# Attention with all softmax row sums made on TensorE, and the next heads' loads issued by ScalarE

## The reference

```
xn = layernorm(x)
q, k, v = split(clip(xn @ Wqkv.T, -8, 8))           # 32 heads of 32
q, k = layer_norm(q)*w + b, layer_norm(k)*w + b
scores = q k^T / sqrt(32) + slope[h] * (key - query); causal mask
probs = softmax(scores);  attn = (probs @ v) @ Wout.T
out = x + attn + xn @ (mean|W| * sign(W)).T + bias
```

## Time and profile before

| what | value |
|---|---|
| three runs | 1596.76, 1600.59, 1603.05 us |
| median | 1600.59 us |
| profiled execution, its own time | 1595.62 us |
| its span, first to last instruction | 1593.8 us |
| mean granted TensorE clock | 0.957 of full |
| PE busy | 1420.4 us (89%) |
| DVE busy | 731.8 us (46%) |
| POOL busy | 615.8 us (39%) |
| ACT busy | 571.5 us (36%) |

### The profile page before, as it was taken

The page is one execution under the profiler, slowest core; times in us unless marked ns, Lnnn a source line. Parts: engine busy times, 40 slices in busy tenths (PEclk is TensorE's granted clock), DMA queues, the critical chain, the costliest instruction groups (busy, mean ns, idle before and its releaser), DMA issues.

```text
span 1593.8 us, 24481 instructions
## 1 busy us (share of the span) xinstructions
PE 1420.4 (89%) x9256; PEld 655.4 (41%) x9256; DVE 731.8 (46%) x1246; ACT 571.5 (36%) x1081; POOL 615.8 (39%) x380
## 2 busy tenths in 40 slices
PE   4899999999999979999988878888988888797998
PEld 2455445444545434444333333333433333233443
DVE  6665355545454311267655555555655555301111
ACT  4443133323333200005555545555555555530000
POOL 4221122222222100003555556666555555666443
PEclk9999999999999989999999999999999999899999
DMA  6453232322232372211222221122222221024543
GB/s 234 152 165 113 66 79 59 79 60 72 67 79 59 93 200 79 80 53 48 69 69 62 65 57 46 47 69 69 70 69 69 62 65 28 17 85 158 158 145 119
DMA packets 145396, 136.85 MB, mean 86 GB/s; under 512 B 83744, under 2 KB 112416, under 8 KB 145120
## 3 DMA queue, kind: packets, MB, share of 16 engines
q1 hardware_dynamic: 79264, 118.92, 25.4%
q10 hardware_dynamic: 66048, 16.78, 4.9%
HBM read 93.06 MB, written 42.47 MB: 85 GB/s over the span
## 4 chain that ended last, share of the span: by engine, by line
PE 56%; POOL 25%; issue 12%; ACT 3%; DMA 2%; DVE 1%; SPq 1%; POOLq 0%; ACTq 0%; DVEq 0%
PE ps L979 38%; POOL arena L588 21%; PE ps L1115 4%; PE ps L1054 4%; PE ps L1138 3%; PE ps L1143 2%; PE ps L1032 2%; ACT arena L721 2%; PE ps L1148 2%; POOL arena L567 1%; PE ps L1057 1%; POOL small L530 1%; DMA v_scr<-arena 1%; PE ps L1118 1%; ACT arena L729 1%
## 5 line engine op out<-in xcount | busy, mean ns | idle before, releaser
L979 PE MATMUL ps<-arena 128*128 128x512 f16 x3584 | 795.9, 382 | 28.7 <-DVE arena L857 9.8
L979 PEld LDWEIGHTS ps<-arena 128*128 128x128 f16 (+1 forms) x3584 | 349.8, 98 | 446.1 <-issue 13.5
L588 POOL TENSOR_TENSOR arena<-arena 128x2048 f32<-128x2048 f32 (+1 forms) x96 | 330.6, 3444 | 473.2 <-ACT arena L721 466.1
L886 DVE TENSOR_REDUCE arena<-ps 128x1 f16<-128x512 f32 (+3 forms) x768 | 380.1, 551 | 282.7 <-PE ps L1057 247.5
L721 ACT ACTIVATE arena<-ps 128x512 f32<-128x512 f32 (+3 forms) x768 | 332.4, 493 | 170.2 <-PE ps L1118 77.8
L1115 PE MATMUL ps<-arena 128*128 128x512 f16 (+3 forms) x768 | 252.2, 337 | 113.6 <-ACT arena L721 111.9
L1054 PE MATMUL ps<-arena 127*128 127x512 f16 (+3 forms) x768 | 240.3, 334 | 0.0
L1115 PEld LDWEIGHTS ps<-arena 128*128 128x128 f16 x768 | 75.4, 99 | 288.6 <-ACT arena L721 189.3
L857 DVE TENSOR_SCALAR arena<-ps 128x1024 f32<-128x1024 f32 x48 | 58.8, 1225 | 253.4 <-PE ps L979 226.1
L1138 PE MATMUL ps<-arena 128*32 128x512 f32 (+3 forms) x1536 | 163.9, 508 | 0.4 <-ACT arena L729 0.2
L555 POOL TENSOR_TENSOR arena<-arena 128x1024 f16<-128x1024 f32 x32 | 68.0, 2125 | 125.4 <-ACT arena L698 125.4
(11 more groups left out here) (51 smaller groups left out, 873.6 us busy)
## 6 DMA issues: line engine op xcount, KB each, us to landing
arena<-in_x SPq DMA_DIRECT2D x32, 512.0 KB, 4.5
arena<-in_wqkv_t SPq DMA_DIRECT2D x48, 256.0 KB, 4.0
base_scr<-arena SPq DMA_DIRECT2D x16, 512.0 KB, 2.8
q_scr<-arena ACTq DMA_DIRECT2D x16, 512.0 KB, 4.1
k_scr<-arena ACTq DMA_DIRECT2D x16, 512.0 KB, 4.4
arena<-k_scr SPq DMA_DIRECT2D x16, 512.0 KB
arena<-q_scr SPq DMA_DIRECT2D x32, 256.0 KB
v_scr<-arena SPq DMA_DIRECT2D x16, 512.0 KB, 2.9
```

The lines of the kernel that those rows point to most:

```text
L588: nc.gpsimd.tensor_tensor(acc[:, :, at:HALF], former, p32[k % PSLOTS][:, :, 0:w], ALU.add)\
L886: ins = nc.vector.tensor_reduce(negm[s % 2][:, at:at + 1], ps[:, NATB[use(s, pos) % RB], col:col + width], AX, ALU.max, negate=True)
L979: ins = nc.tensor.matmul(dst[c], lhs(k, a), wparts[:, k, b, c * HALF:(c + 1) * HALF], start=(k == 0 and (a, b) == order[0]), stop=(k == KT ...
```

## The change

- GpSimd's additions, `acc` and their semaphore are gone. `with_v` multiplies every chunk's exponentials with the ones; the product with `acc` is gone.
- The loads of V and of the stack leave SP. ACT issues them: V of group n+1 behind (2, 3), and the seven parts of the stack of group n+2 one per chunk, behind (3, 3) to (9, 3).
- ACT's `o_high` of the first half moves from (0, 3) to (2, 0), `os_copy` of the second half from (2, 0) to (2, 1), `o_high` of the second half from (8, 1) to (9, 0).
- The tables `NATS` and `PV_AFTER` are new.

```diff
-        acc = f32(at, PW).rearrange("p (j q) -> p j q", j=GH); at += PW
...
-        NATS = [4, 3, 3, 2, 5, 4, 4, 4, 5, 4, 2, 2]
+        NATS = [3, 4, 3, 2, 5, 5, 3, 4, 4, 4, 3, 2]
...
-        PV_AFTER = {(1, 0): [-2], (2, 0): [-1], (2, 3): [0], (4, 2): [1], (5, 2): [2], (6, 2): [3],
...
+        PV_AFTER = {(0, 3): [-2], (2, 1): [-1], (3, 0): [0], (4, 2): [1], (5, 2): [2], (6, 2): [3],
+                    (7, 1): [4], (7, 3): [5], (8, 3): [6], (9, 3): [7, 8], (11, 0): [9]}
...
-        def load_stack(eng, n):
+        LOADS = 7
+
+        def load_part(eng, n, part):
...
             for n in range(STACKS):
-                load_stack(sp, n)
+                for part in range(LOADS):
+                    load_part(sp, n, part)
...
-                    if n < GROUPS - 1:
-                        load_vg(sp, n + 1)
-                    if n + 2 < GROUPS:
-                        sp.wait_ge(st_done, NC * GH * n)
-                        load_stack(sp, n + 2)
...
-            def add_in(n, c):
...
-                nc.gpsimd.tensor_tensor(acc[:, :, at:HALF], former, p32[k % PSLOTS][:, :, 0:w], ALU.add)\
-                  .then_inc(add_done, 1)
-
             for n in range(GROUPS):
                 for c in range(NC):
-                    if not DIRECT[c] and CHUNKS[c][1] > 1:
-                        add_in(n, c)
...
                     need(act, pv_done, k - PSLOTS + 1)
-                    need(act, add_done, adds_for(k - PSLOTS))
...
+                            if (c, j) == (2, 3) and n < GROUPS - 1:
...
+                                load_vg(act, n + 1)
+                            if j == 3 and 3 <= c < 3 + LOADS and n + 2 < GROUPS:
+                                load_part(act, n + 2, c - 3)
...
-                if DIRECT[c]:
-                    for j in range(GH):
-                        ins = nc.tensor.matmul(dst(S_BANK, j, at), ones_w, p[:, j, 0:w],
-                                               start=first, stop=last and qb == 0)
-                if last and qb == 1:
-                    pe.wait_ge(add_done, ADDS * (n + 1))
-                    for j in range(GH):
-                        ins = nc.tensor.matmul(dst(S_BANK, j, 0), ones_w, acc[:, j, :], start=False, stop=True)
+                for j in range(GH):
+                    ins = nc.tensor.matmul(dst(S_BANK, j, at), ones_w, p[:, j, 0:w], start=first, stop=last)
```

More of the change, by code:

```diff
@@ L337, in load_stack @@
             hk = k_scr[h0:h0 + GH, :, toks].rearrange("j r t -> r j t")
[L338 to L342, removed]
-                cols = slice(a * HALF, (a + 1) * HALF)
-                eng.dma_start(qs[s][0:2 * DH, a], hq[:, :, cols]).then_inc(stack_ld[s], 16)
-                eng.dma_start(qs[s][2 * DH:3 * DH, a], hq[0:DH, :, cols]).then_inc(stack_ld[s], 16)
+            if part == 0:
+                dst, src = ks[s][0:DH], hk[0:DH]
+            elif part == 1:
+                dst, src = ks[s][DH:3 * DH], hk
+            elif part == 2:
+                dst, src = ks[s][3 * DH:3 * DH + 3], k_extra[h0:h0 + GH].rearrange("j r t -> r j t")
+            else:
+                a, again = (part - 3) // 2, (part - 3) % 2
+                cols = slice(a * HALF, (a + 1) * HALF)
+                if again:
+                    dst, src = qs[s][2 * DH:3 * DH, a], hq[0:DH, :, cols]
+                else:
+                    dst, src = qs[s][0:2 * DH, a], hq[:, :, cols]
+            eng.dma_start(dst, src).then_inc(stack_ld[s], 16)
         def stack_loaded(n):
-            return 16 * 7 * (n // STACKS + 1)
+            return 16 * LOADS * (n // STACKS + 1)
         def load_vg(eng, n):
@@ L477, in _ @@
                     sums_out(blk_no(n - 1, 1))
-                    if n == 1:
-                        for s in range(2):
-                            sp.wait_ge(v_st[s], stored(NT // 2))
-                    if n < GROUPS - 1:
-                        load_vg(sp, n + 1)
-                    if n + 2 < GROUPS:
-                        sp.wait_ge(st_done, NC * GH * n)
-                        load_stack(sp, n + 2)
                 if n < GROUPS - 1:
@@ L577, in o_low @@
                 nc.gpsimd.tensor_tensor(part[1], os_sb[m % 2][:, 0, :], part[0], ALU.subtract).then_inc(ol_done, 1)
-            def add_in(n, c):
-                qb, t, at, w = span(c)
-                k = n * NC + c
-                pool.wait_ge(exp_done, GH * (k + 1))
-                if t == 2:
-                    need(pool, pv_done, n * NC)
-                need(pool, add_done, adds_for(k) - 1)
-                former = p32[(k - 1) % PSLOTS] if t == 2 else acc[:, :, at:HALF]
-                nc.gpsimd.tensor_tensor(acc[:, :, at:HALF], former, p32[k % PSLOTS][:, :, 0:w], ALU.add)\
-                  .then_inc(add_done, 1)
             for n in range(GROUPS):
                 for c in range(NC):
-                    if not DIRECT[c] and CHUNKS[c][1] > 1:
-                        add_in(n, c)
                     if n > 0:
@@ L597, in _ @@
                             o_norm(n - 1, 0)
-                        if c == 2:
+                        if c == 3:
                             o_low(n - 1, 0)
-                        if c == 6:
+                        if c == 5:
                             o_norm(n - 1, 1)
-                        if c == 9:
+                        if c == 10:
                             o_low(n - 1, 1)
@@ L748, in _ @@
                         if n > 0:
-                            if (c, j) == (0, 3):
+                            if (c, j) == (2, 0):
                                 o_high(n - 1, 0)
-                            if (c, j) == (2, 0):
+                            if (c, j) == (2, 1):
                                 os_copy(n - 1, 1)
-                            if (c, j) == (8, 1):
+                            if (c, j) == (9, 0):
                                 o_high(n - 1, 1)
+                            if (c, j) == (2, 3) and n < GROUPS - 1:
+                                if n == 1:
+                                    for s in range(2):
+                                        act.wait_ge(v_st[s], stored(NT // 2))
+                                load_vg(act, n + 1)
+                            if j == 3 and 3 <= c < 3 + LOADS and n + 2 < GROUPS:
+                                load_part(act, n + 2, c - 3)
                         if (c, j) == (6, 2):
```

7 lines of the change are left out of this document (removed).

## The result

| | median us | lowest to highest | runs |
|---|---|---|---|
| before | 1598.67 | 1595.71 to 1603.05 | 4 |
| changed | 1506.34 | 1504.68 to 1507.80 | 4 |

The ratio is 0.942, with a 95% interval of 0.9392 to 0.9448: faster, by 92.3 us. The profiled execution took 1504.95 us for a span of 1503.1, 90.7 less than the profiled one of before. I had forecast 1520 and a range that began at 1509: the direction is right, the gain larger than I had allowed for. Of the 13.7 us between 1520 and 1506.34, 10.5 lie in the sum (1515.4 against 1504.95). The other 3.2 come from the 5.0 that I added for the distance of the median from the profiled execution: here it is 1.4, and with the fourth run of before it is 3.05 there, so the 5.0 was the distance in one set of three runs and no property of the kernel.

The account below looks back on a forecast made before the run. PE was held up by o_norm queued behind GpSimd's additions; a middle group was to go 44.3 - 7.7 - 2.05 + 3.9 = 38.5 us. In all -80.2 us: 1595.62 to 1515.4, given as 1520 for the median, range 1509 to 1550.

Parts of the forecast that it names:

- What bounds the kernel: Attention stage: PE waits 7.41 us for an exponential because o_norm queues behind GpSimd's additions, not for want of data.
- The wait and the slow stretch: Middle groups: dropping the additions removes 7.66 us of wait and 2.05 us lost at half clock behind it.
- The ones products: PE, per group: 4.74 us of new ones products, less 0.86 for the acc product, net +3.9 us.
- The loads on ACT: DMA issues moved from SP to ACT, covered by with_v: cost nothing, at worst a microsecond for late data.
- The way back: Second half's reciprocals on SP: 5.5 us from store to load taken as unchanged, with 5 us of slack at (9, 0).
- The tables: New NATS and PV_AFTER on PE: items stay 42, every with_v finds its exponentials old enough, so nothing.
- Group 1: The stage's second group goes from 39.5 to 38.5 us, a gain of 1.0 us.
- The signs: Attention stage if right: groups 38 to 39 us apart, PE idle under 1 us, clock 1.00, ones products 0.86 us.
- The first (stalls by issues): DMA issues on ACT stall PE by some 0.3 us each, 2.1 us a group: 1549 us, chance 0.14.
- the second: The wait returns at (9, 0) because the store behind the loads takes longer, 4 us a group: 1576 us, chance 0.06.
- the third: ScalarE (ACT) becomes the bound if an issue holds it 2.8 us, groups of 46.3 us: 1628 us, chance 0.03.
- the fourth: Ones products on PE cost twice their price, 4.74 us more in each of 16 groups: 1596 us, chance 0.03.

Follow-up runs that it names:

- e8: Kernel before, all six additions kept, with o_norm of a group's first half moved ahead of the last two additions in GpSimd's queue: 1572.17 us.
- e4: A with the old NATS and PV_AFTER, and o_high and os_copy back at their old places on ACT: 1511.27 us.
- e7: A with all six additions back on GpSimd, o_norm of the second half ahead of them: 1564.01 us.
- e3: A with the 512-wide ones products of chunks 5, 6 and 7 done twice: 1544.75 us.
- e1: A with the loads of V and stack back on SP at their old place: 1506.97 us.
- e2: A with the seven stack parts issued in one row by ACT behind (4, 3), instead of one per chunk: 1544.62 us.
- e12: A with the old NATS alone: 1512.09 us.
- A: The changed kernel itself, with the whole change against the kernel before: 1506.34 us.
- e5: A with three additions (chunks 5 to 8) back on GpSimd, o_norm of the second half ahead of them: 1501.11 us.
- e11: A with three additions on GpSimd, o_norm of the second half behind all three, o_low and o_high later: 1489.98 us.
- e9: A with three additions on GpSimd, o_norm of the second half behind the first of them: 1467.59 us.

## Why the prediction was right in kind and too small

- **What bounds the kernel.** Right. The chain addition, `o_norm`, `o_high`, exponential, scores was the one long wait, by place in the queue and not by data. e8 shows it by moving one instruction; e4 shows that without the additions `o_high` has no wait at its early place, and e7 that with all six additions PE waits for GpSimd again although `o_high` stands later.
- **The wait and the slow stretch.** 7.66 and 2.05 us were read from one group by the modelled ends. From start to start the two waits are 7.57 and 0.31 and the slow stretch loses 1.93: 9.81 for 9.71, together 0.1 us a group too little. In the last group the 7.8 us that I counted can't be read from the earlier trace rows, which show only the 1.54; the trace has a wait of 7.84 there.
- **The ones products.** +3.9 net, with 0.86 for 512 columns: e3 measured 0.857. Right, and the dearer reading by busy time (1.04) was rightly left to the range; it had no part in the result.
- **The loads on ACT.** "I cost it at nothing": e1 finds nothing, and e2 shows the cover and its limit. I named `with_v` as the cover; the trace shows a nearer one, the activation that the issue runs beside.
- **The way back.** The store's 5.5 us became 3.2, the shorter of the two readings that I weighed, and decided nothing, as said; e1 keeps 5 us and the same time.
- **The tables. This step failed.** "The items stay 42 [...] Nothing." The count was right and the conclusion wrong: the new `NATS` is worth 0.41 us a group by e12. Part of it (0.22) is which product stands next to the row item, part (0.15) a short wait for a bank at chunk 10 that the new table avoids. e12 and e4 are 5.8 and 4.9 us slower than A. With the 0.1 above and 0.1 that I haven't found, that is the 0.6 between 5.85 and 6.46 us. With the old `NATS`, at 1512.09, the measurement would have been inside the range that I gave.
- **Group 1.** I cut its stretch from a window that began 1.3 us into it and ended 0.4 behind it. From first score to first score it was 40.44, not 39.5, and the new group took 37.82, not 38.5: -2.6 for -1.0.
- **The start of the stage** came 1.1 us earlier. The edit touches nothing ahead of it, and in the traces of all runs the stage starts between 719.8 and 724.2 us: it is spread.
- **The range** took in costs that might be dearer and gave only 5 us downward, for the spread of runs; counted from the sum of 1515.4 that is the 1510 of the forecast, and why the range begins at 1509 isn't said. The order of PE's queue was costed at exactly zero, without a bound below. An edit to the order of the bounding engine deserves one on both sides, even where the count of its work stays the same.
- **The signs.** PE without idle time, clock 1.00, `o_norm` waiting for a DMA, `o_high` for nothing, ones products of 0.86: all came, but the groups are 37.82 us apart and not 38 to 39.
- **The rivals** didn't come. The first (stalls by issues) is e2's case, not A's; the second had 6.5 us of room; for the third ACT is busy 23.45 of 37.82; the fourth is refuted by e3.

Still open: 0.04 of the 0.41 us, and 0.1 us a group that no run places; four or six additions with `o_norm` behind the first, which weren't tried.

## What to carry to other kernels

Work on an idle engine is free only if nothing short and urgent stands behind it in that engine's queue, and only if it doesn't itself stand behind something that waits for a DMA: before dropping such work, try a part of it, with the urgent instruction at another place (here three additions of six, 39 us better than none). A row whose instruction has almost no idle time ahead of it, while another engine waits for it, is a place in a queue and not late data. Spread DMA issues on a computing engine one to an activation. When one engine bounds a stage, its order is a cost of its own, even with the same work in it, and where its ends are modelled a short wait can hide in "busy": compare start to start.

## What the chip showed that I had not expected

- A shorter wait can be followed by a longer slow stretch. Behind 7.50 us PE was granted 0.50 for 4.10 us; behind 3.72 us, in e8, for 8.76. In e8 the stretch behind the wait lasted 8.5 to 8.9 us in five middle groups and 5.4 to 6.8 in eight; in before it was 3.3 to 4.5. So half of a wait removed was worth less than half of its price.
- The clock also fell behind a wait of 2.24 us, in e2, in every other group. Two stretches of e2, each from a place in one group to the same place in the next:

```profile
805.33:845.53 40.20, 37.96 (x358) 16.86 (x354) 24.14 (x53) 23.21 (x55) 4.87 (x4) 1.00 0.28 69
845.53:887.32 41.79, 39.55 (x360) 17.43 (x355) 24.33 (x53) 23.61 (x55) 4.87 (x4) 0.96 0.27 66
```

  The idle time is the same 2.24 us in both, and the second is 1.6 us longer by the clock alone. The Trainium skill, TensorE: Matmul & The Clock Gate, in the table of the section Why this matters for your kernels, has the rule that I weighed in the prediction, and it speaks of longer gaps than this; the row shows that a shorter one can cost as well. The measurement decides. The length of the wait doesn't settle it alone: e2's other groups keep 1.00 behind the same 2.24 us, so does e5 behind its waits of 1.58 and 1.71, and in e11 the wait of 1.67 us was followed by 3.4 us at 0.50 in the last group only (from 1276.62).
- A DMA issue on ACT's queue runs beside the activation that has started, but a row of seven holds the next one: 4.3 us, 3.81 of them idle.
- On PE the step from a product with 128 columns of weights to one with 32 (f32) or 16 (f16) is 0.14 to 0.15 us start to start where 0.06 is usual, about 0.09 more, and back from the 16 as well; the one with 16 columns placed ahead of the f32 ones hides in that step. Whether it is the number of columns or the type, no run separates; the row item is f16 and has the step too.
- An addition on GpSimd of 128x2048 takes 4.27 us in the kernel before (12.82 for three) and 4.6 in e5 and e9 (13.89 for three, 9.21 for two). I don't know why.
